# Building the next quad's one-hot matrices behind this quad's additions in the third layer's edge sums

## The reference, cut to what matters

```python
    def _L2_gnn_ref(node_features, edge_index, edge_attr_tensor, ...):
        row, col = (edge_index[0], edge_index[1])
        r_vec = edge_attr_tensor[:, :3]
        dist = edge_attr_tensor[:, 3:4]
        xj = node_features[col]
        s = xj[:, :64]
        v = xj[:, 64:].reshape(e, 32, 3)
        m0 = s @ Wm_ss * dist * INV8 + jnp.einsum('eui,ei->eu', v, r_vec) @ Wm_vv * (INV_SQRT3 * INV_SQRT32)
        m1 = (s @ Wm_sv)[:, :, None] * r_vec[:, None, :] * INV8 + jnp.einsum('eui,uw->ewi', v, Wm_vs) * dist[:, :, None] * INV_SQRT32
        ...
        msg = jnp.concatenate([m0, m1.reshape(e, 96)], axis=-1)
        agg = jax.ops.segment_sum(msg, row, num_segments=n)
```

## Time and profile before

| | |
|---|---|
| time before, median of 3 runs | 11017.17 us (11013.29 to 11042.03) |
| the profiled execution's own time | 11009.26 us |
| its span in the trace | 11007.4 us |
| busy share of the span | PE 72%, DVE 70%, POOL 67%, PE weight loads 53%, ACT 44% |
| the stage's gathers (L1709), first start and last start | 5011.0 and 6142.3 us |
| the next stage's first multiplication on TensorE (L1801) | 6157.39 us |

### The profile page before, as it was taken

The page is one execution under the profiler, slowest core; times in us unless marked ns, Lnnn a source line. Parts: engine busy times, 40 slices in busy tenths (PEclk is TensorE's granted clock), DMA queues, the critical chain, the costliest instruction groups (busy, mean ns, idle before and its releaser), DMA issues. The chain is left out here.

```text
span 11007.4 us, 242155 instructions
## 1 busy us (share of the span) xinstructions
PE 7979.6 (72%) x60118; PEld 5819.1 (53%) x60119; DVE 7733.9 (70%) x25514; ACT 4813.2 (44%) x16219; POOL 7321.4 (67%) x12018
## 2 busy tenths in 40 slices
PE   3222222379996888866677686888888888888887
PEld 1000000057775665644444443777777777777776
DVE  6333333468887666635555487889999899999987
ACT  0000000047774445422222102777767766776775
POOL 2777777777775777726777201777777777777775
PEclk9656555589998999968999897999999999999998
DMA  5111111023332333313333492000000000000000
GB/s 150 29 29 29 29 29 27 20 64 77 78 77 67 73 73 74 73 33 91 89 90 90 96 199 57 21 21 21 21 21 21 21 21 21 21 21 21 21 22 22
DMA packets 828471, 567.96 MB, mean 52 GB/s; under 512 B 588110, under 2 KB 763941, under 8 KB 825674
## 3 DMA queue, kind: packets, MB, share of 16 engines
q0 software_dynamic: 218720, 330.70, 11.1%
q1 hardware_dynamic: 596842, 196.50, 9.8%
q10 hardware_dynamic: 12480, 35.51, 0.9%
HBM read 482.70 MB, written 79.57 MB: 51 GB/s over the span
## 5 line engine op out<-in xcount | busy, mean ns | idle before, releaser
L2440 POOL DMA_INDIRECT l_source_rows<-node_table,l_edge_rows x866 | 854.3, 986 | 948.8 <-DMA l_edge_rows<-rows_by_dst 689.3
L585 PE MATMUL rank<-onehots,upper_h 128*128 128x427 f16 x812 | 368.4, 454 | 1387.3 <-DVE pos L536 1381.0
L535 DVE CUSTOM_DVE_ANT_0 junk<-rank,onehots 128x401 f16<-128x401 f32 x812 | 458.3, 564 | 1166.0 <-POOLq L609 1165.6
L1327 POOL DMA_INDIRECT l1s_tile_rows<-node_table,l1s_tile_rows x864 | 989.0, 1145 | 353.4 <-issue 258.0
L1709 POOL DMA_INDIRECT l2s_node_rows<-node_table,l2s_edge_rows x864 | 869.3, 1006 | 499.2 <-issue 262.7
L605 POOL DMA_INDIRECT rows_by_src<-row_s,pos_i x812 | 782.7, 964 | 431.5 <-issue 427.9
L585 PEld LDWEIGHTS rank<-onehots,upper_h 128*128 128x128 f16 x812 | 81.2, 100 | 1865.2 <-DVE pos L536 1864.2
L908 POOL DMA_INDIRECT l_source_rows<-node_table,l_edge_rows x880 | 871.3, 990 | 279.0 <-issue 206.6
L605 POOL DMA_INDIRECT rows_by_dst<-row_d,pos_i x812 | 784.1, 966 | 267.4 <-issue 267.4
L1722 ACT ACTIVATE l2s_rows_by_edge<-l2s_node_rows,l2s_edge_rows 128x160 f32<-128x160 f32 x864 | 299.2, 417 | 865.8 <-DMA l2s_node_rows<-node_table,l2s_edge_rows 865.8
L1453 ACT COPY l1s_pair_rows<-l1s_tile_rows 128x200 f32 x1240 | 352.4, 355 | 603.4 <-POOLq L1332 583.8
(11 more groups left out here) (580 smaller groups left out, 27093.6 us busy)
## 6 DMA issues: line engine op xcount, KB each, us to landing
l_xv_by<-h_turned_l SPq DMA_DIRECT2D x120, 320.0 KB
l_source_rows<-node_table,l_edge_rows POOLq DMA_INDIRECT x1746
l_xs_by<-h_turned_l SPq DMA_DIRECT2D x40, 640.0 KB
rows_by_src<-pad_rows_s ACTq DMA_DIRECT2D x16, 1053.0 KB
l1s_tile_rows<-rows_by_src SPq DMA_DIRECT2D x216, 78.0 KB
l2s_edge_rows<-rows_by_src SPq DMA_DIRECT2D x216, 78.0 KB
l_edge_rows<-rows_by_dst SPq DMA_DIRECT2D x220, 72.0 KB, 2.0
l_edge_rows<-rows_by_dst SPq DMA_DIRECT2D x433, 36.0 KB
```

What stands on the lines that cost most here:

```text
L535: nc.vector.tensor_tensor_reduce(junk[:, t % SETS, RS], rank[:, 1, t % STREAMS, RS], hots[:, t, RS], 1.0, 0.0, ALU.mult, ALU.add, pos[:, k ...
L1327: pool.indirect_dma_start(ring[:, t, 0:XW], None, table, bass.IndirectOffsetOnAxis(ap=ring[:, t, XW + S_DST:XW + S_DST + 1].bitcast(U32), ...
L2440: pool.indirect_dma_start(xg[u][:, s, :], None, K["table0"], bass.IndirectOffsetOnAxis(ap=pay[u][:, s, D_SRC:D_SRC + 1].bitcast(U32), axis ...
```

## The change

The one-hots leave `build` and become a function `onehots` of their own. In the loop, `build(k)` (now only the two products) is followed by `add(k)` and then by `onehots` for quad q + 1. The one-hots of quad 0 are made ahead of the loop, after the two memsets. `onehots` needs the edge rows alone, so it waits for `pay_in` (the SP load) and for the sums of the quad six before its own, not for gathers. `build` waits for the gathers and for `hot_made`, a new semaphore that `onehots` tells. The last call makes one-hots for a quad 216 that does not exist; SP gets a 217th load of edge rows for it, and nothing uses the result. SP's code moves into a function `load` for that reason. TensorE, ScalarE and POOL keep their code.

```diff
--- before.py
+++ after.py
@@ -1684,18 +1684,22 @@
         pay_in, xg_in = [sem(f"pay_in{k}") for k in range(AHEAD)], [sem(f"xg_in{k}") for k in range(AHEAD)]
         built, scaled, summed, added, pool_seen, pe_seen, sp_seen = (
             sem(n) for n in ("built", "scaled", "summed", "added", "pool_seen", "pe_seen", "sp_seen"))
-        assert LEAD_C == BANKS * HALVES and QUADS % AHEAD == 0 and QUADS * QUAD * P <= ROWS_S
+        assert LEAD_C == BANKS * HALVES and QUADS % AHEAD == 0 and (QUADS + 1) * QUAD * P <= ROWS_S
         with nc.Block() as block:
             @block.sync
             def _(sp):
+                def load(it, k):
+                    sp.wait_ge(built, AHEAD * it + (k + 1))
+                    sp.sem_inc(sp_seen, 1)
+                    sp.wait_ge(scaled, AHEAD * it + (k + 1))
+                    sp.sem_inc(sp_seen, 1)
+                    at = (AHEAD * it + k) * (QUAD * P)
+                    sp.dma_start(pay[k][:, :, :], K["rows_s"][bass.ds(at, QUAD * P), :].rearrange("(s p) w -> p s w", p=P)).then_inc(pay_in[k], 16)
+
                 with sp.Fori(0, ITERS) as it:
                     for k in range(AHEAD):
-                        sp.wait_ge(built, AHEAD * it + (k + 1))
-                        sp.sem_inc(sp_seen, 1)
-                        sp.wait_ge(scaled, AHEAD * it + (k + 1))
-                        sp.sem_inc(sp_seen, 1)
-                        at = (AHEAD * it + k) * (QUAD * P)
-                        sp.dma_start(pay[k][:, :, :], K["rows_s"][bass.ds(at, QUAD * P), :].rearrange("(s p) w -> p s w", p=P)).then_inc(pay_in[k], 16)
+                        load(it, k)
+                load(ITERS, 0)
 
             @block.gpsimd
             def _(pool):
@@ -1744,13 +1748,18 @@
             def _(dve):
                 regs = [dve.alloc_register(f"l2_bin{h}") for h in range(AHEAD * HALVES)]
 
-                def build(k, loaded, free_at):
+                by = lambda c, n, *d: free(c, [n, QUAD], *d)
+
+                def onehots(k, loaded, free_at):
+                    dve.wait_ge(pay_in[k], loaded)
+                    dve.wait_ge(summed, free_at)
+                    nc.vector.tensor_tensor(hot[k % RING][:, :, :], free(K["iota_f"][:, 1:2], [0, QUAD], [1, P]),
+                                            by(pay[k][:, 0, S_LOC:S_LOC + 1], WORDS_S, [0, P]), ALU.is_equal).then_inc(hot_made, 1)
+
+                def build(k, loaded, made):
                     r = k % RING
-                    by = lambda c, n, *d: free(c, [n, QUAD], *d)
                     dve.wait_ge(xg_in[k], loaded)
-                    dve.wait_ge(summed, free_at)
-                    nc.vector.tensor_tensor(hot[r][:, :, :], free(K["iota_f"][:, 1:2], [0, QUAD], [1, P]),
-                                            by(pay[k][:, 0, S_LOC:S_LOC + 1], WORDS_S, [0, P]), ALU.is_equal)
+                    dve.wait_ge(hot_made, made)
                     axes = by(pay[k][:, 0, S_E4:S_E4 + 1], WORDS_S, [1, 3], [0, CV])
                     nc.vector.tensor_tensor(u[r][:, :, D:D + 3 * CV].rearrange("p s (i c) -> p s i c", i=3),
                                             xg[k][:, :, CS:D].rearrange("p s (i c) -> p s i c", i=3), axes, ALU.mult)
@@ -1767,17 +1776,20 @@
                     dve.wait_ge(half_added, HALVES * q + (HALVES * BANKS + HALVES + 1))
                     dve.sem_inc(added, 1)
 
-                half_added = sem("half_added")
+                half_added, hot_made = sem("half_added"), sem("hot_made")
                 for s in (built, scaled, summed):
                     dve.sem_inc(s, AHEAD)
                 nc.vector.memset(p_sum[:, :, :, :], 0.0)
                 nc.vector.memset(acc[:, :, :], 0.0).then_inc(half_added, 1)
                 dve.wait_ge(half_added, 1)
+                onehots(0, 16, 1 + AHEAD - RING)
                 with dve.Fori(0, ITERS) as it:
                     dve.reg_load(regs, bins[0:1, bass.ds(it * (AHEAD * HALVES), AHEAD * HALVES)])
                     for k in range(AHEAD):
-                        build(k, 16 * QUAD * it + 16 * QUAD, AHEAD * it + (k + 1 + AHEAD - RING))
+                        build(k, 16 * QUAD * it + 16 * QUAD, AHEAD * it + (k + 1))
                         add(k, AHEAD * it + (k - BANKS))
+                        n = k + 1
+                        onehots(n % AHEAD, 16 * it + 16 * (n // AHEAD + 1), AHEAD * it + (n + 1 + AHEAD - RING))
                 dve.reg_load(regs[0:BANKS * HALVES], bins[0:1, ITERS * AHEAD * HALVES:(ITERS * AHEAD + BANKS) * HALVES])
                 for k in range(BANKS):
                     add(k, ITERS * AHEAD + (k - BANKS))
```

## The result

The changed kernel takes 10973.07 us (median of 6 runs, 10971.09 to 10977.82) against 11019.72 us for the kernel before (6 runs, 11011.49 to 11042.03). The ratio is 0.9955, with a 95% interval of 0.9944 to 0.9966: 46.7 us less by the medians. 10971 us was forecast.

What follows compares the result with a forecast made beforehand. POOL's issuing of gathers was taken as the bound. Terms -51 + 2 + 1 + 2 = -46 us take the profiled 11009.26 to 10963; the median lies 7.9 us above that execution, giving 10971 us, range 10960 to 11003.

Steps and rivals of the forecast that it cites:

- The bound: In the changed stage POOL's issuing of 864 gathers bounds, 1132 us; waits of PE and VectorE are slack.
- the 51 us: Excess gather length in this stage: gathers starting while VectorE works on two SBUF operands are held; all 51 us can go.
- Where the gathers fall: In the new order all four gathers of a quad start clear of two-operand instructions; third free by 0.06 us at least.
- rival 1: One-hots land on the fourth gather, 0.5 us a quad: +59 us, 11076 us; chance 0.06.
- heads: Loop's head, 18 times: first product slightly late, 0.1 us a head, 2 us lost, 16 as the other end.
- start: Stage start, VectorE catching up behind its memsets: some gathers held, 1 us of loss, bounds 0 to 4.
- scatter: Scatter of the landings: a few quads in a hundred lose 0.4 us, 1 to 3 us, taken as 2.
- the end: Last one-hots to next stage: same VectorE work in another order, 0 within 0.5 us.
- The base: Profiled execution of the kernel before, 11009.26 us, with the median of the runs 7.9 us above it.
- rival 2: Nothing gained: POOL's long gathers have another cause or are held by something moving with the landing; 11017 us, chance 0.08.
- rival 3: Half comes back through loop heads or a shifted lag holding third gathers: -10 to -32, about 10995 us; chance 0.13.

Runs made afterwards that it cites:

- the order alone: Kernel before with 352-column multiplications left out and own quad's one-hots moved behind the additions, nothing made ahead: 10982.87 us, ratio 0.9956 to the full kernel before.
- the prefetch alone: Changed kernel with 352-column multiplications left out and next quad's one-hots made between products and additions: 11064.57 us, ratio 1.0031 to the full kernel before.
- the third and the fourth run: Changed kernel plus one extra comparison a quad behind the one-hots, second operand in SBUF (third) or PSUM (fourth): 12612 and 12601 us, ratios 1.0004 and 1.0.
- the first comparison: Changed kernel against the kernel before, 6 runs each: 10973.07 against 11019.72 us, ratio 0.9955.
- the last four runs: Kernels before, changed, order alone and prefetch alone, each without the 352-column multiplications: 11023.65, 10975.26, 10982.87 and 11064.57 us.
- the eight runs between: One-hot order, prefetch and extra-comparison variants, one-hots sooner, second-layer product cut in four, and two repeats: ratios to kernel before 0.9996 to 1.0004, cut one 1.0096.
- the light kernels: Four kernels (before, changed, order alone, prefetch alone) with this stage's 352-column multiplications left out: 11023.65, 10975.26, 10982.87 and 11064.57 us.
- light changed kernel: Changed kernel with this stage's 352-column multiplications left out: 10975.26 us, ratio 0.9953 to the full kernel before.

## Why the prediction was right, point by point

**The bound.** Right. POOL waits for nobody before and after, and the 352-column multiplications taken out change nothing that can be measured (11023.65 against 11029.56 us, ratio 0.9998, 0.9988 to 1.0007). The 0.6 us by which TensorE starts sooner are worth nothing.

**The cause of the 51 us.** Right, and now shown: two instructions that differ in one operand's place (0.25 us a gather against 0.001), the order alone (1083.3 us) and the prefetch alone (1164.9 us). By the rule of the Trainium skill that speaks against it (page "SBUF — State Buffer", section "Who interferes with whom", tensor_tensor does not stall DMAs that GpSimd describes) the third and the fourth run's extra instruction should have held no gather. The one with two SBUF operands did (61 gathers, 15.1 us), so the inference does not hold for these gathers. The other sentence of that section of the Trainium skill, that such an instruction contends with a GpSimd instruction that reads SBUF, agrees with these traces. They show the hold and what it depends on; that a shared port is the reason is the Trainium skill's explanation, and no run tests it.

**Where the gathers fall.** Right. The one-hots were forecast at 2.68 and stand there to the hundredth; third and fourth gather were forecast at 1.18 and 2.43, and in the quad above are found at 1.14 and 2.39. Over the quads of the steady part (the 21st to the 212th) the third has its median at 1.08 and the fourth at 2.33, since the lag of the landing has its median at 2.68 and not at the 2.57 of the quad that was read. That lies within the 2.5 to 2.8 allowed for, but the third gather's margin behind the products was thinner than worked out: the earliest start is 0.84, and that gather is 0.07 us longer. No fourth gather came later than 2.51 there, so none ran into the one-hots, and rival 1 did not come.

**The terms of the sum.** Forecast were -51 + 2 (heads) + 1 (start) + 2 (scatter) = -46 us. Measured from the gathers, 48.9 us are gone (869.3 to 820.4) and some 3 are left, 820.4 - 0.946 x 864. Of these 1.8 lie in the first 14 quads, where VectorE catches up; the forecast for the start was 1 us of new loss on top of 1. Some 0.4 us lie in the last nine quads. The heads cost nothing measurable. The 2 us for them rest on 2.45 + 2.6 = 5.05 to 5.15, while the working ahead of it (2.44 and some 0.1) gives 2.45 + 2.54 = 4.99. Measured, the first product starts 2.66 us behind the additions' end at a head (median), since the register load (1.61 us) starts 0.5 us into the one-hots and runs beside their last part only. The lag is 2.72 there against 2.67 elsewhere, so the first product is 0.05 us late. Behind the first head, while VectorE still catches up, one gather is 0.30 us longer; behind the others none is. The scatter costs below 1 us. So the stage gained 2.8 us more than the sum (48.8 against 46). At the end nothing was won or lost worth naming: last gather to next stage 14.7 us (6099.12 to 6113.79) against 15.1 (6142.32 to 6157.39).

**The base.** The medians moved by 46.7 us, the stage in the profiled executions by 48.8. The two profiled executions themselves differ by only 33.6 us (11009.26 to 10975.62). The rest is in stages whose code is the same: the stage's first gather came 5.6 us later, and some 10 us more are lost behind it. I take that as scatter between single executions: the profiled one of the kernel before was faster than all six others. The medians carry the verdict. That 10971 came within 2 us of 10973.07 is in part luck, since the stage's 2.8 us, the head's wrong sum and the scatter of the base are all of that size.

**The forecast of no gain (rival 2) and of half a gain (rival 3)** did not come. No gain was measured all the same in the runs in which TensorE was the bound, for a reason that the prediction didn't name.

## What to carry to other kernels

Where POOL issues indirect DMAs back to back and waits for nobody, compare the mean length of one with the median; an excess may be VectorE instructions with two SBUF operands that run when a DMA is issued. Their place against POOL's rhythm can then be worth more than their number: put instructions with a PSUM operand where the issues fall. Cutting a long one shortens the hold (0.13 against 0.55 us a gather), but the one kernel in which it was tried, with TensorE as the bound, got slower. A change of order is priced by laying both engines' starts on one time axis, and only by a trace in which the bound is the one that the change works on.

## What was not expected of the hardware

TensorE behaved in two ways in one and the same kernel. In the first comparison and beside the last four runs the kernel before took 11020 to 11030 us. Beside the eight runs between it took 12491 to 12608 us, and the traces of those runs have a granted clock of 0.80 to 0.82 in this stage where 1.00 stood before. Stretches of 8 to 11 us (the medians of the eight traces; 4 to 19 us singly) in which single multiplications start 1 to 3.5 us apart come every 24 to 35 us (medians), and the usual pace, or half of it for a few microseconds, lies between. The whole gain of 47 us vanishes in it. The eight runs were on three chips; the one that had it in two of them did not have it in the light kernels' runs later. What brings it on is not known.

The Trainium skill (page "TensorE: Matmul & The Clock Gate", section "Seeing it yourself") tells of a limiter of peak current that takes a whole die to 13/16 of the clock when a third core of it runs dense multiplications. By that section of the Trainium skill the clock is held there while the load lasts. The measured 0.80 lies near that, but no run here shows what other cores did, and these traces show crawl and usual pace in turn.

In the light kernels TensorE was granted 0.50 of its clock throughout this stage, the lower of its two levels (1.2 GHz of 2.4), and it still kept up: 160 of 512 columns at half of the clock, and the stage no longer. The stretch is that of the light changed kernel:

```profile
5200.00:6000.00 800.00, 394.29 (x1276) 334.85 (x1276) 480.40 (x800) 221.47 (x640) 605.13 (x640) 0.50 0.39 94
```

The second layer's sums hold far more than this stage did: in the changed kernel 286 of 864 gathers start in one product of 1.22 us and are 174.6 us longer together. A stretch of it, as it stands after the change:

```profile
3552.57 1.22 DVE L1360 TENSOR_TENSOR l1s_edge_by_node<-l1s_pair_rows,l1s_edge_by_node 128x1024 f32<-128x1024 f32 x1
3553.13 1.49 POOL L1327 DMA_INDIRECT l1s_tile_rows<-node_table,l1s_tile_rows  x1 [0.30 <-issue]
3554.92 0.95 POOL L1327 DMA_INDIRECT l1s_tile_rows<-node_table,l1s_tile_rows  x1 [0.30 <-issue]
```

The gather ends at 3554.62, 0.83 us behind the product. How much of the 174.6 us could be had there, with TensorE 83% busy (3600 to 4700 us), stays open.
